# VectorE releases each quad to TensorE, root products move behind quads 24 to 48, and GpSimd waits for its own rows behind every fourth or second quad

## Chip, cores and metric
The kernel runs on one core of a Trainium2 chip. The metric is the device time of one execution in microseconds (us), as the median of several executions. For the kernel before it is 6669.53 us, of 3 executions between 6668.03 and 6680.55 us.

## What is computed
A graph of 3125 nodes with 128 features and 50000 edges (sorted by their target node) goes through four residual blocks; each adds its output to its input and normalises the sum:

```python
x = _layernorm(x + L0(x, edge_index, edge_weight, ...))     # 3 layers: weighted mean of neighbours
x = _layernorm(x + L1(x, edge_index, edge_attr_64, ...))    # message network over nodes and edge features
x = _layernorm(x + L2(x, edge_index, edge_type_8, ...))     # 2 relational convolutions
x = _layernorm(x + L3(x, node_type_16, edge_type_32, ...))  # 2 layers of attention
# in each layer of L0
agg = segment_sum(e_w[:, None] * h[src], dst)
out = relu(agg / clip(segment_sum(e_w, dst), 1) @ w_neigh.T + h @ w_root.T + b_root)   # then a layer norm
# in L2
xt = einsum('ni,rio->nro', x, W);  out = segment_sum(xt[src, etypes], dst) + x @ Wl + b
```

Eight times in all (3 + 1 + 2 + 2 layers) the kernel reads, for every edge, a row of a table by the edge's source, and sums over the edges of each target node.

## The kernel before
**Tiles, quads and steps.** The nodes are 25 blocks of 128 (`NB`). The edges are 391 tiles of 128 (`EDGE_TILES`). One step multiplies one tile of gathered rows with a one-hot matrix (edge by target node within a block) on TensorE and adds the product to a block of an accumulator in PSUM (`accf`, all 25 blocks at once); a tile whose edges reach over two blocks takes two steps, so there are 416 steps. Four tiles are a quad of tiles (98 of them, `TILE_QUADS`), four steps a quad of steps (104, `ALL_QUADS`). `trips` loops over 16 steps (4 quads of steps).

**A gather pass.** All eight passes use `gathers` (L438) on GpSimd: 391 indirect DMAs (L449), one per tile, each of 128 rows, into a ring of 60 tiles (`RING`) in `arena`. Ahead of every fourth tile from tile 60 on it calls `freed`, which waits until the tiles that are to be overwritten have been used (in most passes the semaphore `quad_done` of TensorE). The rows of quad k report to a semaphore `gathered[k % 16]`; `hand_over(k)` waits for it and then counts `arrived` up by one, which is what the consumers wait for. The quad handed over after tile t is the one before the quad just issued, so that GpSimd waits for rows whose transfer was started at least four tiles earlier. The last two are handed over after the loop.

**The order of the passes.** Passes 0, 1 and 2 are the three layers of L0, pass 3 is L1, passes 4 and 5 are the two convolutions of L2, passes 6 and 7 the two attention layers of L3 (`score_phase`). Between two passes the accumulator is turned into the next table, which is stored to memory and must be complete before the next pass gathers from it.

**Passes 0, 1, 2, 4 and 5** are `aggregate_phase` (L654). VectorE makes the one-hots (`onehots`, L427 for all four of a quad at once, L431 one by one where the edge weight is multiplied in), up to 12 quads ahead of TensorE (`DEEP`), and counts `onehot_ready`. TensorE, per quad of steps, waits for `onehot_ready`, then reads from a table in SBUF how many quads of tiles must have arrived (`step_need`, L477, a register load with its checks), waits for `arrived` against that register, and issues four products (L717), each a weight load and a matmul. In pass 0 (`sums`) it also adds the edge weights up, one product per quad (L485). In passes 4 and 5 (`root`) 25 root products (L681, x times Wl, one per block) stand ahead of the quad loop, behind the products that fill the accumulator with the bias (L534).

**Passes 1 and 2** (`edges`, class `EdgeShare`) carry besides, quad by quad, a part of the edge network of L1: TensorE (L816, L835, L822), ScalarE (L856, L867, L871) and VectorE (`mix`, L888) hand each other half a bank, and SyncE loads and stores. `join` calls `mix` for quad n-2 behind the one-hots of quad n; TensorE's products for quad n-2 (`output`, L822) stand in its quad n and wait until quad n-1 is mixed.

**Pass 3** adds the rows on VectorE (L1176) and multiplies on TensorE (L1213). **Passes 6 and 7** gather two rows' width, make scores on VectorE (L1857), and SyncE stores the values (L1840) from the ring, eight transfers per quad; `freed` there waits for these stores too.

## Time and profile before
| | us |
|---|---|
| median of 3 executions | 6669.53 |
| the profiled execution | 6655.79 |
| its span (first to last instruction) | 6654.1 |
| PE busy in it | 3255.9 (49%) |
| DVE busy in it | 2193.3 (33%) |
| ACT busy in it | 1125.8 (17%) |
| POOL busy in it | 3207.3 (48%) |
| DMA packets' mean | 116 GB/s |

PE is TensorE, DVE VectorE, ACT ScalarE, POOL GpSimd, SP SyncE. Register, branch, semaphore and DMA-issuing instructions are not counted as busy, except that POOL's indirect DMAs are (the time in which it makes their descriptors). All of these are means over the whole program, in which the eight gather passes and the stages between them differ; the stretches have to be read one by one.

### The profile page before, as it was taken

The numbers are of one execution on the slowest core, as the hardware profiler recorded it, in microseconds if no ns is written. First come the engines' busy times: TensorE is split into PE (matmuls) and PEld (weight loads), VectorE is DVE, ScalarE is ACT, GpSimd is POOL, SyncE is SP. The second block draws the span as 40 slices with busy tenths as digits, with TensorE's granted clock in tenths as the row PEclk, the third lists the DMA queues.
The fourth block names the chain that finished last, engine by engine and source line by source line (L and its number), as shares of the span: only waits on it lengthen the run. The fifth ranks groups of instructions, "written<-read, shape, count | busy, mean of one in ns | idle before, by whom it ended". The sixth has DMA issues, their size and how long they took to land. (4 is left out here: it accounts for less than half of the span.)

```text
span 6654.1 us, 60476 instructions
## 1 busy us (share of the span) xinstructions
PE 3255.9 (49%) x14685; PEld 2293.0 (34%) x14685; DVE 2193.3 (33%) x5075; ACT 1125.8 (17%) x2416; POOL 3207.3 (48%) x3406
## 2 busy tenths in 40 slices
PE   5444477747773445543353335633334256234353
PEld 3333355534452233332332322223334222233343
DVE  3112222322223223411121114423348544233485
ACT  0000122222222111100010002300114323001053
POOL 4664566446643665366546652066630420666302
PEclk7666676767776667665575557766667677666676
DMA  2111333323332332211131127944434489444343
GB/s 60 47 46 34 79 101 100 93 66 100 102 99 73 94 93 69 106 45 46 42 126 47 46 60 308 408 118 126 128 103 117 137 322 394 117 127 129 99 130 104
DMA packets 600928, 772.14 MB, mean 116 GB/s; under 512 B 89734, under 2 KB 507000, under 8 KB 588064
## 3 DMA queue, kind: packets, MB, share of 16 engines
q1 hardware_dynamic: 480000, 492.16, 22.0%
q0 software_dynamic: 120608, 276.12, 15.6%
q8 instruction: 152, 2.49, 0.2%
q14 instruction: 168, 1.38, 0.1%
HBM read 416.10 MB, written 351.82 MB: 115 GB/s over the span
## 5 line engine op out<-in xcount | busy, mean ns | idle before, releaser
L449 POOL DMA_INDIRECT arena<-table,idx_s x3128 | 2986.5, 955 | 2487.2 <-issue 887.8
L717 PE MATMUL ps<-arena,work 128*128 x4160 | 940.1, 363 | 906.9 <-issue 853.4
L717 PEld LDWEIGHTS ps<-arena,work 128*128 128x128 f32 x4160 | 786.5, 261 | 1163.7 <-issue 1162.0
L431 DVE TENSOR_SCALAR work<-iota_row,dl_s,w_s 128x128 f32<-128x128 f32 x1248 | 347.3, 356 | 446.5 <-remote 330.9
L1897 PE MATMUL ps<-ident,onehot 128*128 128x128 f32 x832 | 193.6, 377 | 614.1 <-DVE onehot L427 385.6
L1857 DVE TENSOR_TENSOR arena<-arena,ps 128x128 f32<-128x128 f32 x832 | 183.8, 282 | 822.1 <-remote 623.2
L427 DVE TENSOR_TENSOR work<-ps,dl_s 128x512 f32<-128x512 f32 x208 | 137.4, 688 | 948.2 <-remote 652.7
L888 DVE SCALAR_TENSOR_TENSOR arena<-ps,vecs,arena 128x256 f32<-128x256 f32 x208 | 100.6, 484 | 965.3 <-ACT arena L867 497.1
L1908 PE MATMUL ps<-arena 128*128 x1664 | 331.4, 363 | 168.3 <-issue 108.7
L1908 PEld LDWEIGHTS ps<-arena 128*128 128x128 f32 x1664 | 298.2, 269 | 201.4 <-issue 198.9
L1897 PEld LDWEIGHTS ps<-ident,onehot 128*128 128x128 f32 x832 | 135.2, 194 | 645.8 <-DVE onehot L427 402.3
L1777 PE MATMUL ps<-arena,work 32*128 32x512 f32 x1600 | 303.5, 887 | 98.3 <-DVE work L1801 45.2
L1805 DVE COPY arena<-ps 128x1024 f32<-128x1024 f32 x200 | 238.8, 1221 | 271.2 <-DMA table<-arena 184.8
L485 PE MATMUL ps<-work,picks 128*104 128x512 f32 x416 | 276.1, 737 | 97.1 <-issue 93.8
L1886 ACT ACTIVATE arena<-ps 128x512 f32<-128x512 f32 x208 | 122.9, 597 | 1140.9 <-remote 658.7
L1612 POOL DMA_INDIRECT sorted_x<-work,pos_i x50 | 48.7, 973 | 548.7 <-DVE work L1704 534.1
L816 PE MATMUL ps<-arena 128*128 128x256 f32 x416 | 190.1, 550 | 219.4 <-issue 112.2
L822 PE MATMUL ps<-arena 128*128 128x128 f32 x832 | 199.4, 378 | 188.1 <-issue 127.3
L1213 PE MATMUL ps<-work,arena 128*128 128x128 f32 x832 | 160.9, 317 | 266.7 <-issue 263.6
L1213 PEld LDWEIGHTS ps<-work,arena 128*128 128x128 f32 x832 | 144.4, 229 | 347.5 <-issue 347.5
L1792 ACT ACTIVATE arena<-ps 128x1024 f32<-128x1024 f32 x200 | 197.9, 1022 | 310.5 <-DMA table<-arena 210.2
L1176 DVE TENSOR_TENSOR arena<-arena 128x128 f32 x416 | 103.8, 289 | 389.2 <-issue 370.2
(329 smaller groups left out, 4077.5 us busy)
## 6 DMA issues: line engine op xcount, KB each, us to landing
table<-arena SPq DMA_DIRECT2D x96, 2048.0 KB
values<-arena SPq DMA_DIRECT2D x832, 64.0 KB
arena<-values SPq DMA_DIRECT2D x208, 256.0 KB
arena<-table,idx_s POOLq DMA_INDIRECT x3128
arena<-edge_times SPq DMA_DIRECT2D x208, 128.0 KB
edge_part<-arena SPq DMA_DIRECT2D x208, 128.0 KB
table<-arena SPq DMA_DIRECT2D x50, 512.0 KB
arena<-edge_part SPq DMA_DIRECT2D x98, 256.0 KB
```

The source lines that it names most:

```text
L431: is_dst = dve.tensor_scalar(home[:, at + c, :], iota, dl_s[:, ds(j + c, 1)], weight[:, ds(j + c, 1)], ALU.is_equal, ALU.mult)
L449: pool.indirect_dma_start(ring[:, ds(t % RING * 2 * H, width)], None, tab, bass.IndirectOffsetOnAxis(ap=idx_s[:, t:t + 1], axis=0)).then_i ...
L485: mm = pe.matmul(quad_sums, picks[:, ALL_QUADS - n:2 * ALL_QUADS - n], deep[:, 4 * (n % DEEP):4 * (n % DEEP) + 4, :].rearrange("p c e -> p ...
L717: mm = pe.matmul(accf[:, ds(b, P)], o, ring[:, ds(slot, H)], start=False, stop=False, skip_group_check=True)
L816: pe.matmul(self.half_b, self.We2, self.hid[:, r, :], start=True, stop=True, skip_group_check=True).then_inc(turned.sem, 1)
L822: mm = pe.matmul(self.half_a[:, c * P:(c + 1) * P], self.ef[:, r, c * P:(c + 1) * P], self.Wn1b, start=True, stop=True, skip_group_check=True)
L1213: mm = pe.matmul(accf[:, ds(b, P)], relu_h[:, (i * U + u) % (4 * RELUS), :], o, start=False, stop=False, skip_group_check=True)
L1777: mm = pe.matmul(ps[:, 4 * kv + g, :], (value_ring if kv else key_ring)[rows, b % 2, :], (pair_v if kv else pair_k)[rows, half * 16:(half ...
L1792: act.activation(rows32[:, m % 3, :, kv * H:kv * H + 64].rearrange("p t (g c) -> p g t c", g=2), ps[:, 4 * kv:4 * kv + 2, :].rearrange("p ...
L1805: dve.tensor_copy(rows32[:, m % 3, :, kv * H + 64:(kv + 1) * H].rearrange("p t (g c) -> p g t c", g=2), ps[:, 4 * kv + 2:4 * kv + 4, :].re ...
L1897: mm = pe.transpose(ps[:, q % 2, c * P:(c + 1) * P], onehot[:, 4 * q + c, :], ident[:, :])
L1908: mm = pe.matmul(ps[:, 4 + q, c * P:(c + 1) * P], onehotT[:, q % 2, c * P:(c + 1) * P], Qn_flat[:, ds(b, P)], start=True, stop=True)
```

## The change
It has five parts. (1) `gathers` gets a number `rest`: behind every `rest`-th quad of tiles it hands over the quad just issued as well, and so waits for its rows before it issues the next DMA. `rest` is 4 in passes 0, 3, 4 and 5 and 2 in passes 1, 2, 6 and 7. (2) In `aggregate_phase` VectorE, behind the one-hots of quad n, reads the need, waits for `onehot_ready` and `arrived` and counts a new semaphore `step_ready` (`release_steps`); TensorE waits for `step_ready` alone, against a constant (in pass 0 for `onehot_ready` too, ahead of the sum). (3) `join` calls `mix` for quad n-1 instead of n-2, behind the release of quad n. (4) The 25 root products stand one by one behind the quads 24 to 48. (5) The base of `step_ready` is moved on after each such pass.

```diff
@@ gathers
-        def gathers(pool, tab, width, freed, joins=None):
+        def gathers(pool, tab, width, freed, joins=None, rest=4):
+            handed = [0]
...
-                if t % 4 == 3 and t >= 7:
-                    hand_over(t // 4 - 1)
-            for k in range((EDGE_TILES - 4) // 4, TILE_QUADS):
+                if t % 4 == 3:
+                    done = t // 4 + 1
+                    for k in range(handed[0], done if done % rest == 0 else done - 1):
+                        hand_over(k)
+                        handed[0] = k + 1
+            for k in range(handed[0], TILE_QUADS):
                 hand_over(k)
...
+        def release_steps(dve, n):
+
+            need = step_need(dve, n)
+            dve.wait_ge(onehot_ready.sem, onehot_ready.at(n + 1))
+            dve.wait_ge(arrived.sem, need + arrived.base)
+            dve.sem_inc(step_ready.sem, 1)
@@ aggregate_phase
-                    gathers(pool, tab, H, freed)
+                    gathers(pool, tab, H, freed, rest=2 if edges else 4)
...
-                    onehots(dve, weight, edges.join if edges else None, iota=None if edges or sums else iota_ps, home=deep)
+                    def then(i, q, first):
+                        release_steps(dve, i * QUADS + q)
+                        if edges:
+                            edges.join(i, q, first)
+                    onehots(dve, weight, then, iota=None if edges or sums else iota_ps, home=deep)
...
-                    if root is not None:
-                        for b in range(NB):
-                            pe.matmul(accf[:, b * P:(b + 1) * P], XT[:, b * P:(b + 1) * P], root, start=False, stop=False,
-                                      skip_group_check=True)
+
+                    def root_product(b):
+
+                        pe.matmul(accf[:, b * P:(b + 1) * P], XT[:, b * P:(b + 1) * P], root, start=False, stop=False, skip_group_check=True)
...
-                                pe.wait_ge(onehot_ready.sem, onehot_ready.at(i * QUADS + u // 4 + 1))
                                 if sums:
+                                    pe.wait_ge(onehot_ready.sem, onehot_ready.at(i * QUADS + u // 4 + 1))
                                     quad_total(pe, i * QUADS + u // 4)
-                                pe.wait_ge(arrived.sem, step_need(pe, i * QUADS + u // 4) + arrived.base)
+                                pe.wait_ge(step_ready.sem, step_ready.at(i * QUADS + u // 4 + 1))
...
                                 mm.then_inc(quad_done.sem, 1)
+                                if root is not None and ROOT_FROM <= i * QUADS + u // 4 < ROOT_FROM + NB:
+                                    root_product(i * QUADS + u // 4 - ROOT_FROM)
@@ EdgeShare
-                if not (first and q < 2):
-                    self.mix(nc.vector, i * QUADS + q - 2, q % 2, not first)
+                if not (first and q < 1):
+                    self.mix(nc.vector, i * QUADS + q - 1, (q - 1) % 2, not (first and q < 3))
...
-                for m in range(ALL_QUADS - 2, ALL_QUADS):
-                    self.mix(dve, m, m % 2, True, m == ALL_QUADS - 1)
+                self.mix(dve, ALL_QUADS - 1, (ALL_QUADS - 1) % 2, True, True)
@@ L1 (pass 3)
-                    gathers(pool, table, H, freed, joins)
+                    gathers(pool, table, H, freed, joins, rest=4)
@@ score_phase (passes 6 and 7)
-                        gathers(pool, table32, 2 * H, freed)
+                        gathers(pool, table32, 2 * H, freed, rest=2)
```

How the instructions stand, in three places. `ISA` are register and semaphore instructions without a name of their own, `xN` is N in a row, and a wait stands on the instruction that follows it.

GpSimd at the start of pass 0 (`rest` 4), before:

```order
L449 DMA arena<-table,idx_s 128x128 x8
L449 DMA arena<-table,idx_s 128x128 [waits gathered0]
L449 DMA arena<-table,idx_s 128x128 x3
L449 DMA arena<-table,idx_s 128x128 [waits gathered1]
L449 DMA arena<-table,idx_s 128x128 x3
L449 DMA arena<-table,idx_s 128x128 [waits gathered2]
```

and now:

```order
L453 DMA arena<-table,idx_s 128x128 x8
L453 DMA arena<-table,idx_s 128x128 [waits gathered0]
L453 DMA arena<-table,idx_s 128x128 x3
L453 DMA arena<-table,idx_s 128x128 [waits gathered1]
L453 DMA arena<-table,idx_s 128x128 x3
L453 DMA arena<-table,idx_s 128x128 [waits gathered2,gathered3]
L453 DMA arena<-table,idx_s 128x128 x7
```

Behind the sixteenth tile the wait is for quads 2 and 3, and quad 3 is the one just issued; then seven DMAs follow before the next wait.

TensorE at the start of pass 4's quad loop, before:

```order
L534 MATMUL ps<-brow,ones 128x128
L681 MATMUL ps<-wts,work 128x128 x25
L465 TENSOR_LOAD blk_i
L466 ISA x2
L472 TENSOR_LOAD slot_i
L473 ISA x2
L477 TENSOR_LOAD need_i [waits onehot_ready]
L477 ISA x2
L711 REGISTER_ALU
L717 ISA [waits arrived]
L717 MATMUL ps<-arena,work 128x128
```

and now at one of the quads 24 to 48:

```order
L735 ISA [waits step_ready]
L735 MATMUL ps<-arena,work 128x128
L735 ISA
L735 MATMUL ps<-arena,work 128x128
L735 ISA
L735 MATMUL ps<-arena,work 128x128
L735 ISA
L735 MATMUL ps<-arena,work 128x128
L700 MATMUL ps<-wts,work 128x128
```

The load of the need, its two checks and the addition are gone from each quad of TensorE, and one root product stands behind each of these 25 quads.

VectorE at the start of pass 0, before (the first twelve quads of one-hots, then one quad at a time):

```order
L431 TENSOR_SCALAR work<-iota_row,dl_s,w_s 128x128 x48
L431 TENSOR_SCALAR work<-iota_row,dl_s,w_s 128x128 [waits quad_done]
L431 TENSOR_SCALAR work<-iota_row,dl_s,w_s 128x128 x3
L431 TENSOR_SCALAR work<-iota_row,dl_s,w_s 128x128 [waits quad_done]
L431 TENSOR_SCALAR work<-iota_row,dl_s,w_s 128x128 x3
```

and now:

```order
L433 TENSOR_SCALAR work<-iota_row,dl_s,w_s 128x128 x4
L484 TENSOR_LOAD need_i
L484 ISA x2
L433 TENSOR_SCALAR work<-iota_row,dl_s,w_s 128x128 [waits onehot_ready,arrived]
L433 TENSOR_SCALAR work<-iota_row,dl_s,w_s 128x128 x3
```

Each quad of one-hots now stands behind the wait for the rows of the quad before it.

## Rows read from the trace of the kernel before

**Rows 1.** The page, busy time by engine and the costliest group.

```profile
PE 3255.9 (49%) x14685; PEld 2293.0 (34%) x14685; DVE 2193.3 (33%) x5075; ACT 1125.8 (17%) x2416; POOL 3207.3 (48%) x3406
...
L449 POOL DMA_INDIRECT arena<-table,idx_s x3128 | 2986.5, 955 | 2487.2 <-issue 887.8
```

**Rows 2.** L449 by pass (0, 1, 3, 4, 6): min/median/max ns, first/last start.

```profile
L449 POOL DMA_INDIRECT arena<-table,idx_s x391: 942/947/1096, 64.4 to 615.2; - x196
...
L449 POOL DMA_INDIRECT arena<-table,idx_s x391: 942/947/1070, 682.2 to 1267.4; - x196
...
L449 POOL DMA_INDIRECT arena<-table,idx_s x391: 943/947/1393, 2066.6 to 2626.1; - x196
...
L449 POOL DMA_INDIRECT arena<-table,idx_s x391: 942/947/3378, 2734.3 to 3300.7; - x196
...
L449 POOL DMA_INDIRECT arena<-table,idx_s x391: 943/949/975, 4325.4 to 4925.6; - x196
```

**Rows 3.** Who POOL waited for in pass 4: us in total, times, longest.

```profile
POOL arena L449 <- issue: 107.9, 354, 0.3
...
POOL arena L449 <- remote: 52.5, 13, 5.5
POOL arena L449 <- PE ps L717: 24.2, 5, 19.5
```

**Rows 4.** Timeline of pass 4 (start us, us, engine, line), around a stall.

```profile
2935.13 0.37 PE L717 MATMUL ps<-arena,work 128*128 x1 [1.74 <-issue]
...
2937.89 0.95 POOL L449 DMA_INDIRECT arena<-table,idx_s  x1 [0.31 <-issue]
2938.62 0.37 PE L717 MATMUL ps<-arena,work 128*128 x1 [3.12 <-issue]
2939.32 0.29 PEld L717 LDWEIGHTS ps<-arena,work 128*128 128x128 f32 x1 [2.51 <-issue]
...
2942.13 0.37 PE L717 MATMUL ps<-arena,work 128*128 x1 [1.04 <-issue]
2942.82 0.29 PEld L717 LDWEIGHTS ps<-arena,work 128*128 128x128 f32 x1 [1.11 <-issue]
2943.52 4.72 PE L717 MATMUL ps<-arena,work 128*128 x19 [1.02 <-issue]
...
2943.79 0.94 POOL L449 DMA_INDIRECT arena<-table,idx_s  x1 [4.96 <-remote]
```

**Rows 5.** L717 in passes 0, 1, 4: busy us, mean ns, idle before.

```profile
L717 PE MATMUL ps<-arena,work 128*128 x832 | 168.4, 319 | 244.0 <-issue 242.5 <-POOLq L445 0.9
...
L717 PE MATMUL ps<-arena,work 128*128 x832 | 184.0, 359 | 3.4 <-issue 3.4
...
L717 PE MATMUL ps<-arena,work 128*128 x832 | 201.2, 392 | 321.0 <-issue 288.6 <-DVE work L427 25.5 <-POOLq L445 6.0
```

**Rows 6.** Timeline of pass 0, a short pause of POOL.

```profile
204.05 0.95 POOL L449 DMA_INDIRECT arena<-table,idx_s  x1 [1.63 <-issue]
...
208.71 0.37 PE L717 MATMUL ps<-arena,work 128*128 x1 [1.73 <-issue]
...
211.51 1.23 PE L717 MATMUL ps<-arena,work 128*128 x5 [1.02 <-issue]
```

**Rows 7.** Timeline of pass 1, a short pause of POOL.

```profile
916.47 0.95 POOL L449 DMA_INDIRECT arena<-table,idx_s  x1 [1.38 <-remote]
...
918.36 0.47 ACT L867 ACTIVATE arena<-ps,vecs 128x256 f32<-128x256 f32 x1 [6.24 <-remote]
```

**Rows 8.** DMA, 40 slices of 3301.5 to 3304, behind pass 4's last gather.

```profile
DMA  0000000000000969040201000000000000000000
```

**Rows 9.** Who POOL waited for, pass 6.

```profile
POOL arena L449 <- DMA values<-arena: 91.6, 21, 16.7
```

**Rows 10.** Lines of pass 4 and of pass 1: busy us, mean ns, idle.

```profile
L427 DVE TENSOR_TENSOR work<-ps,dl_s 128x512 f32<-128x512 f32 x104 | 68.8, 688 | 472.2 <-remote 338.6 <-PE ps L717 114.6 <-issue 18.8
...
L681 PE MATMUL ps<-wts,work 128*128 128x128 f32 x50 | 10.5, 368 | 16.8 <-issue 16.6
...
L431 DVE TENSOR_SCALAR work<-iota_row,dl_s,w_s 128x128 f32<-128x128 f32 x414 | 116.4, 353 | 0.0
```

More of the change, by code:

```diff
@@ L54 @@
 RELUS = 10
+ROOT_FROM = 24
 class Signal:
@@ L176, in build @@
         onehot_ready = signal("onehot_ready")
+        step_ready = signal("step_ready")
         quad_done = signal("quad_done")
@@ L746, in aggregate_phase @@
             gather_pass_over()
+            step_ready.base += ALL_QUADS
             if sums:
```

## Prediction

> **What bounds the kernel now.** I first read the page. No engine is half busy [rows 1], but line L449, the indirect DMAs of GpSimd (POOL), has 3128 pieces of 955 ns, 2986 us of a span of 6654. So I went through the program by gather pass. One gather costs 947 ns, and where POOL waits for nothing there are 107.9 / 354 = 0.305 us between two [rows 2, 3]. A pass of 391 gathers issued back to back would last 390 x 1.252 = 488.3 us from the first start to the last. The passes take 550.8 (0), 585.2 (1), 559.5 (3), 566.4 (4) and 600.2 us (6) [rows 2]; pass 2 is built as 1, pass 5 as 4, pass 7 as 6, and I count them the same. Over the floor they are 62, 97, 71, 78 and 112 us. This excess, some 695 us over all eight, is what the change can win or enlarge; the stages between the passes it leaves alone.
>
> What is the excess? In pass 4 it is 52.5 us of waits ended by a remote event and 24.2 us for TensorE's products [rows 3]: both are `freed`, which waits for tiles of the ring to be used up. So TensorE, whose work is small, is late. The timeline shows how [rows 4]: while POOL issues, TensorE does one load or matmul and then idles 1 to 3 us, put down to "issue", that is to nothing that the trace sees. Its steps are multiples of 0.70 us (2938.62 to 2939.32, 2942.13 to 2942.82 to 2943.52). POOL has been quiet from 2938.84, and at 2943.52, 4.7 us later, TensorE suddenly does 19 matmuls in 4.7 us. Over pass 4 this is 288.6 us of idle time ended by "issue" ahead of 832 matmuls, in pass 0 242.5 us [rows 5]. I call it the slow mode: with POOL issuing without a break, another engine's sequencer goes down to one instruction per 0.7 us. In pass 1, where TensorE does more, the same line idles 3.4 us in all [rows 5]. What differs is that POOL there stops every four to eight tiles, for 1.2 to 2.5 us. One such case: POOL stands still from 915.1 to 916.5, and ScalarE, held for 6.24 us by an event that came late, goes on at 918.36 although POOL is issuing again [rows 7]. So a short stop seems to release what was held. Against it stands pass 0: a stop of 1.63 us before 204.05 did not end a slow stretch that lasted until 211.51 [rows 6]; but that stretch had been let grow first.
>
> **Part 1, the waits for own rows.** Behind pass 4's last gather (start 3300.7, end 3301.6) packets move until slice 22 of 40, 3302.9 us [rows 8], 1.2 to 1.3 us. A wait for the rows just issued takes that plus the way back to POOL, in place of the usual 0.305 us: at least 0.9 us more, at most about 1.5; I take 1.2. In passes 0, 3, 4 and 5 there are 24 such waits: 29 us each, floor 488.3 + 29 = 517. In passes 1, 2, 6 and 7 there are 48: 57.6 us, floor 546. SP's and the other queues carry nothing behind POOL, but every consumer waits for `arrived`, which POOL counts; the quad just issued is now handed over earlier than before (before its four successors), the others as before.
>
> What they may win: with a stop each 16 tiles (20 us) or each 8 (11 us), TensorE has few instructions between two stops, and the slow mode, which ends at each long stop and comes again while POOL issues, should not set in. Then the stalls of `freed` go, as TensorE is short of nothing else. I leave 4 us per pass for what remains. Pass 0: 551 - 521 = **30**. Pass 3: 559.5 - 521 = **38**. Passes 1 and 2: 585 - 550 = 35 each, **70**. Passes 4 and 5: 566.4 - 521 = 45 each, **90** (with parts 2 and 4). Passes 6 and 7 wait for SyncE's stores, 91.6 us [rows 9]. SyncE is held in the same way but within a few tiles, so stops every eight tiles end it and do not prevent it; between nothing (600) and all (550) I take 585, nearer the row of before: 15 each, **30**.
>
> **Part 2, VectorE releases.** TensorE loses four register instructions of some 25 records per quad. In the slow mode that is 2.8 us of a quad, outside it nothing, since POOL's 5.0 us per quad (4 x 1.252) covers it. VectorE gains about seven. Its one-hots are 0.69 us per quad (pass 4) or 4 x 0.353 = 1.4 us (pass 1) [rows 10], `mix` under 0.5. The register load has no row on VectorE: between 0 and, at 0.7 us for each of seven, 4.9 us. I take 1 us, as an engine that isn't slow spends well under 0.2 us on such an instruction between TensorE's matmuls of rows 4's fast stretch. Sum 1.4 + 1.0 + 0.5 = 2.9 of 5.0 us: covered. If the cover goes (the 4.9), 1.4 + 4.9 + 0.5 = 6.8 us per quad, and VectorE is the bound. The one-hots ahead of time are lost: what waits behind VectorE's wait is the next quad's one-hots and `mix`, at most 1.9 us behind the rows, inside the 5 us until the next rows. 0.
>
> **Part 3, mix one quad earlier.** It stays opposite TensorE's products of the same quad, without which VectorE, no longer ahead, would hold TensorE. 0.
>
> **Part 4, root products.** Line L681's 50 records (25 products, some in two passes of the array) cost 10.5 us and 16.8 us of idle ahead of pass 4's first quad [rows 10]; POOL pays for it with the 19.5 us at tile 60 [rows 3]. That stall is part of the 45 above. Placed behind quads 24 to 48 they add about 0.4 us to quads that have 5 us. 0 more.
>
> **Sum.** 30 + 38 + 70 + 90 + 30 = 258 us. Against the profiled execution: 6655.8 - 258 = 6398. The median of the runs shown is 13.7 us above that execution; with it, **6410 us**.
>
> **Rivals.**
> (a) *The stops take the place of stalls, but the slow mode stays.* For it: rows 6, and 4.7 us from POOL's stop to TensorE's recovery in rows 4, where a stop of 1.5 us is three times shorter. Then the 29 us of stops are absorbed in the 62 to 78 us of waits, TensorE is quicker only by its missing instructions, and passes 4 and 5 save most of the 19.5 us: some 2 x 25 + 2 x 15 = 80 us, 6590.
> (b) *Nothing much*: absorbed, and the late root products and VectorE's releases eat the rest: within 13 us of 6669.5 (62 us of excess in pass 0 less 29 of stops is a bound on what may be left over there, and in pass 1 97 less 57.6, so that little is left once VectorE's part costs a third of it).
> (c) *The stops come on top: slower.* The place is the loop of POOL and ring in the four passes with `rest=2` above all. If late events still come, and each stop is added in full, that is 4 x 57.6 + 4 x 28.8 = 346 us; the half of it, with the gain of 80 from (a) kept, gives 6670 + 173 - 80 = 6763. It decides when a stop removes less than it costs: 1.2 us per 8 tiles is 57.6 of the 97 us of excess in pass 1, so over 40% of the excess must stay; in pass 0, 29 of 62. For it: pass 1 shows no slow mode on line L717 now, so its stops have less to cure. Against: pass 1's existing waits are of the stop's own length and can merge with it. The Trainium skill speaks for this rival: "DMA: Bandwidth & Descriptors", § Rules for kernel authors, has a DMA issued early and its semaphore waited for late, so that the fixed cost overlaps. The change does the opposite at every drain; by that rule alone the whole 346 would be lost. Rows 4 show why I give it little: POOL idles 4.96 us in one go there already, four times what a stop adds.
> (d) *VectorE becomes the bound: slower.* If its register instructions fall into the slow mode, 104 quads of steps at 6.8 us are 707 us in passes 1 and 2 instead of 550, and at 1.4 + 4.9 us 655 us in pass 0 instead of 521: 6410 + 2 x 157 + 134 = 6858. Against: with stops, nobody should be slow.
>
> **Numbers.** Forecast 0.66 (own range 6330 to 6520), (a) 0.12, (b) 0.07, (c) 0.10, (d) 0.05. A measurement of this kernel can tell about 0.2% (13 us) from no change. Faster: 0.66 + 0.12 = 0.78; same 0.07; slower 0.15. The forecast's low end: all 288 stops at 0.9 instead of 1.2 us give 86 us more, 6324, and passes 6 and 7 may win more than 15 each; the range runs from 6300 to 6680, over (a) and (b), and leaves out (c), (d) and little else.
>
> **What would show it.** Right: line L449's passes at about 521 (0, 3, 4, 5), 550 (1, 2) and 585 us (6, 7); TensorE's idle ended by "issue" ahead of line L735 down from 243 and 289 us to under 60, most of its idle being for VectorE's release; no wait of POOL for TensorE at tile 60 over 5 us; stops of 1.5 us. Wrong: pauses of 4 to 5 us still there between the stops (a, c), VectorE's one-hots 0.7 us apart or later than the rows (d).

## The result: 6504.27 us, 0.975 of before

The changed kernel takes 6504.27 us (median of 4 executions, 6496.06 to 6516.86), the kernel before 6668.78 us beside it (4 executions, 6666.06 to 6680.55). The ratio is 0.9751, 95% interval 0.9734 to 0.9769: 164.5 us faster. 260 had been forecast, and 6410 us. The profiled execution of the change takes 6516.86 us, its span is 6515.1 us, 139.0 less than that of the profiled execution before. What is read from the traces below therefore adds up to 139 us, not to 164.5.

From here on "slow mode" is what the prediction calls so: one instruction per 0.7 us on TensorE, VectorE or SyncE while POOL issues. One thing has to be known to read all that follows. The kernel before took about 6669, 6722 and 6666 us on three of the occasions on which kernels were run for this document, and 5758, 5758 and 5760 us on three others. The traces on the first three show the slow mode, those on the others do not. The result above belongs to the first kind. On record are chips 8 and 4 for the other two occasions with the slow mode, chip 7 once and chip 11 twice for those without it, and none for the result above. The kernel before was traced with the slow mode only; without it, its time and the traces of its variants are known.

### The profile after

The page's busy lines of the change, in answer to [rows 1]:

```profile
PE 3454.9 (53%) x14685; PEld 2426.0 (37%) x14685; DVE 2199.7 (34%) x5075; ACT 1126.3 (17%) x2416; POOL 3210.2 (49%) x3406
...
L453 POOL DMA_INDIRECT arena<-table,idx_s x3128 | 2989.8, 956 | 2458.4 <-issue 995.9
```

TensorE is busy 199 us longer for the same 14685 matmuls; POOL's gathers cost the same. "Issue" ahead of them has grown from 888 to 996 us, which holds a part of the stops; most are put down to line L453's own DMAs, 477 us in 218 waits. Line L453 (the old L449) by pass, 0, 1, 3, 4 and 6, as in [rows 2] (min/median/max ns, first and last start):

```profile
L453 POOL DMA_INDIRECT arena<-table,idx_s x391: 938/944/1094, 64.3 to 618.2; - x196
...
L453 POOL DMA_INDIRECT arena<-table,idx_s x391: 938/944/1052, 678.2 to 1274.1; - x196
...
L453 POOL DMA_INDIRECT arena<-table,idx_s x391: 938/944/1489, 2010.0 to 2575.1; - x196
...
L453 POOL DMA_INDIRECT arena<-table,idx_s x391: 938/944/3577, 2661.9 to 3222.0; - x196
...
L453 POOL DMA_INDIRECT arena<-table,idx_s x391: 940/946/972, 4229.8 to 4837.9; - x196
```

First start to last start is 553.9, 595.9, 565.1, 560.1 and 608.1 us, where it was 550.8, 585.2, 559.5, 566.4 and 600.2. The forecast had 521, 550, 521, 521 and 585. So the passes have hardly moved, most of them the wrong way. The whole program by pass, worked out from the starts and ends of that line (pass: first start to last end; rest: from there to the next pass's first gather, or the end):

| pass | before: pass + rest | after: pass + rest | difference |
|---|---|---|---|
| 0 | 551.8 + 66.0 | 554.9 + 59.0 | -3.9 |
| 1 | 586.1 + 97.1 | 596.9 + 54.7 | -31.6 |
| 2 | 589.1 + 112.1 | 603.5 + 76.7 | -21.0 |
| 3 | 560.4 + 107.3 | 566.1 + 85.8 | -15.8 |
| 4 | 567.3 + 77.7 | 561.1 + 70.8 | -13.1 |
| 5 | 562.6 + 383.5 | 552.4 + 383.6 | -10.1 |
| 6 | 601.2 + 723.5 | 609.1 + 688.2 | -27.4 |
| 7 | 603.6 + 400.4 | 615.2 + 372.8 | -16.0 |

The eight passes together are 37 us **longer**, and the rests between them 176 us **shorter**. The time was won where the prediction said that the change leaves everything alone. Of the 139 us, passes 1, 2, 3, 6 and 7 with their rests have 112, and 0, 4 and 5 have 27.

Why, is seen behind the last gather of a pass. Before, what TensorE still has to do then, in pass 1 (L717) and pass 3 (L1213), and what SyncE still has to store in pass 6 (L1840): count, min/median/max ns, first and last start. Each product is two of these matmuls, so 116 are 58 steps, about a full ring.

```profile
L717 PE MATMUL ps<-arena,work x116: 275/275/581, 1268.8 to 1321.7; 128*128 x116
...
L1213 PE MATMUL ps<-work,arena x140: 269/275/417, 2626.9 to 2658.7; 128*128 128x128 f32 x140
...
L1840 SPq DMA_DIRECT2D values<-arena x59: 4/331/2065, 4928.0 to 4973.3; - x59
```

And after, the same lines under their new numbers:

```profile
L735 PE MATMUL ps<-arena,work x20: 275/421/581, 1275.2 to 1285.1; 128*128 x20
...
L1233 PE MATMUL ps<-work,arena x24: 275/275/422, 2575.8 to 2582.9; 128*128 128x128 f32 x24
...
L1860 SPq DMA_DIRECT2D values<-arena x11: 4/329/341, 4838.9 to 4846.1; - x11
```

116 matmuls that end 53 us behind the last gather have become 20 that end 10 us behind it; 140 (32 us) have become 24 (7 us); 59 stores (47 us) have become 11 (7 us). Before, GpSimd ended a pass with a ring full of rows that nobody had used. Now the consumers have kept up, and since the next pass's table needs the last product, this is worth its full length. They have not only ended closer to GpSimd but earlier: from a pass's first gather to the end of its last product, pass 1 takes 640 us before and 607 now.

The slow mode itself, by line of TensorE (busy, mean ns, idle before): first the kernel before, in pass 1 ahead of the edge network's products and in pass 3:

```profile
L822 PE MATMUL ps<-arena 128*128 128x128 f32 x408 | 98.5, 381 | 84.9 <-issue 60.0 <-DVE arena L888 24.9
...
L816 PE MATMUL ps<-arena 128*128 128x256 f32 x206 | 95.2, 555 | 116.2 <-issue 63.4 <-ACT arena L856 52.0
...
L1213 PE MATMUL ps<-work,arena 128*128 128x128 f32 x832 | 160.9, 317 | 266.7 <-issue 263.6 <-ACT arena L1191 3.1
```

Then the change, for L735 in passes 0, 1 and 4 as in [rows 5], and for L1233 in pass 3:

```profile
L735 PE MATMUL ps<-arena,work 128*128 x832 | 172.4, 332 | 204.2 <-issue 203.3
...
L735 PE MATMUL ps<-arena,work 128*128 x832 | 196.4, 378 | 73.7 <-issue 47.4 <-DVEq L529 26.3
...
L735 PE MATMUL ps<-arena,work 128*128 x832 | 193.4, 373 | 321.6 <-issue 310.1 <-DVEq L529 10.5
...
L1233 PE MATMUL ps<-work,arena 128*128 128x128 f32 x832 | 174.2, 374 | 229.4 <-ACT arena L1211 144.3 <-issue 85.1
```

In passes 0 and 4 it is still there, with the stops: 203 and 310 us of "issue" idle (243 and 289 before). In pass 3, "issue" is down from 264 to 85 us, and TensorE waits most for ScalarE. In pass 1 the slow mode was there before as well, though not ahead of L717, the line that the prediction looked at (3.4 us): it stood ahead of L816 and L822. All of TensorE's idle time ended by "issue", from a pass's first gather to its last, for passes 0 to 7: 288, 127, 121, 307, 296, 326, 164 and 168 us before; 269, 80, 47, 93, 318, 316, 69 and 62 in the change. It has gone down by 37 to 70% in passes 1, 2, 3, 6 and 7, and by 7% at most, if at all, in 0, 4 and 5. (Without the slow mode, the change has 49 us in pass 0 and 1 to 7 in the others.) What POOL waited for in pass 4, in answer to [rows 3]:

```profile
POOL arena L453 <- issue: 138.5, 366, 2.5
...
POOL arena L453 <- PE ps L735: 12.7, 5, 4.0
POOL arena L453 <- remote: 8.1, 4, 4.1
```

The remote waits went from 52.5 to 8.1 us and the products' from 24.2 to 12.7 with 4.0 us as the longest instead of 19.5, but "issue" rose by 31 and the waits for line L453's own rows from 5.5 to 25.2: the stops stand where the stalls stood. One stop in pass 3's timeline:

```profile
2146.48 0.94 POOL L453 DMA_INDIRECT arena<-table,idx_s  x1 [0.30 <-issue]
2149.76 0.94 POOL L453 DMA_INDIRECT arena<-table,idx_s  x1 [2.34 <-DMA arena<-table,idx_s]
2151.01 0.94 POOL L453 DMA_INDIRECT arena<-table,idx_s  x1 [0.30 <-issue]
```

The gap is 2.34 us instead of 0.30: a stop costs **2.04 us** more, not 1.2. Over all stops of the change the median gap is 2.37 to 2.44 us in passes 0 to 5 and 2.73 in passes 6 and 7, whose rows are twice as wide. The transfer took 1.2 to 1.3 us behind pass 4's last gather [rows 8]; if it takes as long here, some 1.1 us pass between its last packet and the next gather's start.

### The profile page after: what moved, and what is told of

Same layout as the page of the kernel before. It is cut to its first block and busy times, and to the rows that moved or that the text cites. A ratio compares the mean times of both kernels' runs of the same rounds, so it can differ in the third digit from the quotient of the medians.

```text
span 6515.1 us, 60996 instructions
## 1 busy us (share of the span) xinstructions
PE 3454.9 (53%) x14685; PEld 2426.0 (37%) x14685; DVE 2199.7 (34%) x5075; ACT 1126.3 (17%) x2416; POOL 3210.2 (49%) x3406
## 5 line engine op out<-in xcount | busy, mean ns | idle before, releaser
L453 POOL DMA_INDIRECT arena<-table,idx_s x3128 | 2989.8, 956 | 2458.4 <-issue 995.9
L735 PE MATMUL ps<-arena,work 128*128 x4160 | 968.1, 370 | 953.0 <-issue 884.8
L735 PEld LDWEIGHTS ps<-arena,work 128*128 128x128 f32 x4160 | 815.3, 269 | 1207.8 <-issue 1207.4
L1917 PE MATMUL ps<-ident,onehot 128*128 128x128 f32 x832 | 217.7, 413 | 671.5 <-DVE onehot L429 543.5
L1928 PE MATMUL ps<-arena 128*128 x1664 | 391.4, 413 | 5.1 <-issue 3.6
L1928 PEld LDWEIGHTS ps<-arena 128*128 128x128 f32 x1664 | 352.7, 313 | 26.5 <-issue 17.1
L492 PE MATMUL ps<-work,picks 128*104 128x512 f32 x416 | 320.8, 857 | 77.8 <-issue 76.8
L1233 PE MATMUL ps<-work,arena 128*128 128x128 f32 x832 | 174.2, 374 | 229.4 <-ACT arena L1211 144.3
L843 PE MATMUL ps<-arena 128*128 128x128 f32 x832 | 218.1, 407 | 135.5 <-DVE arena L909 95.4
L1233 PEld LDWEIGHTS ps<-work,arena 128*128 128x128 f32 x832 | 149.6, 269 | 368.1 <-issue 368.1
```

The source lines that it names most:

```text
L453: pool.indirect_dma_start(ring[:, ds(t % RING * 2 * H, width)], None, tab, bass.IndirectOffsetOnAxis(ap=idx_s[:, t:t + 1], axis=0)).then_i ...
L492: mm = pe.matmul(quad_sums, picks[:, ALL_QUADS - n:2 * ALL_QUADS - n], deep[:, 4 * (n % DEEP):4 * (n % DEEP) + 4, :].rearrange("p c e -> p ...
L735: mm = pe.matmul(accf[:, ds(b, P)], o, ring[:, ds(slot, H)], start=False, stop=False, skip_group_check=True)
L843: mm = pe.matmul(self.half_a[:, c * P:(c + 1) * P], self.ef[:, r, c * P:(c + 1) * P], self.Wn1b, start=True, stop=True, skip_group_check=True)
L1233: mm = pe.matmul(accf[:, ds(b, P)], relu_h[:, (i * U + u) % (4 * RELUS), :], o, start=False, stop=False, skip_group_check=True)
L1917: mm = pe.transpose(ps[:, q % 2, c * P:(c + 1) * P], onehot[:, 4 * q + c, :], ident[:, :])
```

## The experiments

Each takes the changed kernel as its base, unless it says otherwise. `RESTS` gives `rest` by pass, and 1000 means no stop; every other part of the change is kept. The runs stand in order; kernels of one occasion share the executions of the kernel before.

### No stops; stops alone; root products ahead; other stops by pass

```diff
+RESTS = [1000, 1000, 1000, 1000, 1000, 1000, 1000, 1000]
@@ gathers
+        passes = [0]
...
+            rest = RESTS[passes[0]]
+            passes[0] += 1
             handed = [0]
```

> The changed kernel without any wait for own rows (the rest is kept: VectorE's releases, mix a quad earlier, late root products). Theory S (the stops keep the other engines quick, so that nobody is behind when GpSimd has done its last gather): most of the 164 us are lost, 6600 to 6680 us; TensorE ends over 25 us behind the last gather again in passes 1, 2 and 3, and SyncE over 35 us behind in passes 6 and 7. Rival R (TensorE's fewer instructions bring the gain, and the stops only cost): about as fast as the change or faster, 6300 to 6520 us.

The second has the kernel before as its base, with the new loop of `gathers` and `RESTS = [4, 2, 2, 4, 4, 4, 2, 2]`, and nothing else of the change.

> The kernel before with the stops alone (4 quads in passes 0, 3, 4, 5, 2 in 1, 2, 6, 7). Theory S: passes 3, 6 and 7 as in the changed kernel, since the change does nothing else there; passes 1 and 2 close to it; in all 6500 to 6600 us. Rival R: slower than before, 6680 to 6800 us.

```diff
@@ aggregate_phase (third kernel)
                     fill_rows(pe, row)
+                    if root is not None:
+                        for b in range(NB):
+                            root_product(b)
...
-                                if root is not None and ROOT_FROM <= i * QUADS + u // 4 < ROOT_FROM + NB:
-                                    root_product(i * QUADS + u // 4 - ROOT_FROM)
```

> The changed kernel with the 25 root products ahead of the quad loop again, as before. Both theories: only passes 4 and 5 move, by 5 to 20 us each; the stall of GpSimd at tile 60 grows from 3.4 us in pass 4 to over 8 us. In all 6510 to 6540 us.

```diff
+RESTS = [1000, 1000, 4, 2, 1000, 2, 4, 3]
```

> The changed kernel with other stops by pass: none in passes 0, 1 and 4, behind every fourth quad in 2 and 6, every third in 7, every second in 3 and 5. A look at each pass from its first gather to the next pass's. Theory S: pass 1 without stops 20 to 35 us longer than the 651.6 us of the change; pass 2 about the same or 10 us shorter than 680.2; pass 6 between 1297 (change) and 1325 (before); pass 0 and 4 without stops within 10 us of the change's 613.9 and 631.9, as TensorE's steps of 0.7 us are still there with stops; pass 5 with twice as many stops either loses TensorE's 0.7 us steps and is 5 to 25 us shorter, or is up to 40 us longer. Rival R: passes 0, 1 and 4 without stops 20 to 60 us shorter.

Measured: the kernel before 5758.40 us (13 executions, 5755.47 to 5764.98). Without stops 5759.53 us, ratio 1.0001 (0.9991 to 1.001). The stops alone on the kernel before 6426.48 us, 1.1157 (1.1139 to 1.1176). Root products ahead 6425.73 us, 1.1152 (1.1133 to 1.1171). Other stops by pass, one execution, 6147.74 us.

All four expectations missed, since all had 6669 us in mind. Line L458 of the kernel without stops, in passes 1 and 6:

```profile
L458 POOL DMA_INDIRECT arena<-table,idx_s x391: 940/944/1057, 600.6 to 1089.3; - x196
...
L458 POOL DMA_INDIRECT arena<-table,idx_s x391: 942/946/972, 3727.8 to 4215.3; - x196
```

488.7 and 487.5 us from first to last start: the floor of 390 x 1.252 = 488.3 that the prediction worked out, without one stall. Passes 3 (517.0) and 4 (494.5) have no stall either; some of their gathers are longer. Its TensorE in passes 0 and 4:

```profile
L740 PE MATMUL ps<-arena,work 128*128 x832 | 163.2, 359 | 138.2 <-DVEq L534 138.2
...
L740 PE MATMUL ps<-arena,work 128*128 x832 | 203.1, 425 | 246.6 <-DVEq L534 241.9 <-issue 4.7
```

4.7 us of "issue" in pass 4 instead of 289 [rows 5]; TensorE waits for VectorE's release. In the timeline of pass 4 the release comes from VectorE right behind the rows, and all of a quad's eight matmuls follow within 2.07 us while POOL issues:

```profile
2506.06 0.69 DVE L430 TENSOR_TENSOR work<-ps,dl_s 128x512 f32<-128x512 f32 x1 [4.26 <-POOLq L454]
...
2506.13 2.07 PE L740 MATMUL ps<-arena,work 128*128 x8 [3.43 <-DVEq L534]
...
2507.19 0.95 POOL L458 DMA_INDIRECT arena<-table,idx_s  x1 [0.30 <-issue]
```

So on this chip there was nothing for a stop to mend. TensorE's granted clock is not what tells the two kinds apart: in pass 4 its mean was 0.58 of full speed in the trace of before, with the slow mode, and 0.52 here. The kernels then differ by their stops alone: 668.1 us for the 288 stops on the kernel before, 2.32 us each; (6147.74 - 5759.53) / 176 = 2.21 us each for those of the fourth kernel. The other parts (VectorE's releases, `mix`, the late root products) are worth nothing here, 5759.5 against 5758.4, and whether the root products stand ahead or behind makes no difference (6425.7 against 6424.1 and 6415.7 for the change, below): POOL never gets to wait for the ring.

### The change and no stops, once more

> The changed kernel itself, since in the first four runs the kernel before took 5758 us where it had taken 6669, and showed no slow mode. If that belongs to the chip (or to its condition at the time) and not to the kernels, there are two cases. Without the slow mode: before about 5758 us, the change about 6420 us, 288 stops at 2.1 to 2.4 us more each. With it: before about 6669 us, the change about 6500 us.

> The changed kernel without stops, beside the change itself. Without the slow mode: equal to before, about 5758 us. With it: theory S says 6600 to 6680 us, with TensorE over 25 us and SyncE over 35 us behind the last gather; rival R, by which TensorE's fewer instructions brought the gain, says 6300 to 6520 us.

Another chip, and again no slow mode. The change 6415.71 us, ratio 1.1143 (1.1125 to 1.1162) to a before of 5758.34; without stops 5756.86 us, 0.9998 (0.9988 to 1.0007). The difference of the two is 658.9 us, 2.29 us a stop. Who POOL waited for in pass 0 of the change there:

```profile
POOL arena L453 <- issue: 106.7, 344, 0.9
POOL arena L453 <- DMA arena<-table,idx_s: 63.5, 46, 2.5
```

The own rows' waits are put down to line L453's DMAs, 63.5 us with 2.5 as the longest, and beside "issue" and the wait ahead of the pass's first gather there is no other entry. So the change that made this kernel 2.5% faster on one occasion makes it 11.4% slower on another, and its stops are all of the loss. What they cost by pass can be read here without a disturbance: against the kernel without stops, 2.1 us a stop in passes 0, 4 and 5, 2.2 in 1 and 2, 1.9 in 3, and 2.6 in 6 and 7.

### Stops in some passes only, and a later wait in two

```diff
+RESTS = [1000, 1000, -2, 1000, 1000, -4, 1000, 2]
...
-                if t % 4 == 3:
-                    done = t // 4 + 1
-                    for k in range(handed[0], done if done % rest == 0 else done - 1):
+                if t % 4 == (0 if rest < 0 else 3):
+                    done = (t + 1) // 4
+                    for k in range(handed[0], done if done % abs(rest) == 0 else done - 1):
```

> The changed kernel without stops in passes 0, 1, 3, 4 and 6, with them behind every second quad in 7, and in 2 and 5 with a wait for own rows that stands one gather later (behind the first gather of the next quad; every second quad in 2, every fourth in 5). First to last gather start of each pass, and the way to the next pass's first. If the chip shows no slow mode: 488 us in passes 0, 1, 4 and 6, about 518 in pass 3; 613 in pass 7; with the later wait a stop costs about 0.9 instead of 2.1 us, as one gather's 1.25 us lie in it: some 532 us in pass 2, 510 in pass 5. If it does: theory S says pass 3, without stops, has its 0.7 us steps on TensorE and VectorE again and ends 25 us behind the last gather, pass 6 has SyncE over 35 us behind and pass 7 under 10; rival R says passes 1, 4 and 6 are quicker than in the change.

This chip showed the slow mode: before 6721.74 us (3 executions), this 6657.23 us (2), ratio 0.9903 (0.9869 to 0.9936). Passes 1, 3, 4 and 6, all without stops:

```profile
L458 POOL DMA_INDIRECT arena<-table,idx_s x391: 938/944/1053, 679.8 to 1270.3; - x196
...
L458 POOL DMA_INDIRECT arena<-table,idx_s x391: 938/944/1441, 2071.2 to 2638.5; - x196
...
L458 POOL DMA_INDIRECT arena<-table,idx_s x391: 938/944/3808, 2751.2 to 3310.5; - x196
...
L458 POOL DMA_INDIRECT arena<-table,idx_s x391: 940/946/972, 4319.8 to 4944.8; - x196
```

What TensorE still had to do behind the last gather in pass 1 (no stops) and pass 2 (the later wait), and, in a fence of its own, what SyncE had in pass 7 (stops as in the change):

```profile
L740 PE MATMUL ps<-arena,work x112: 275/275/582, 1275.5 to 1325.7; 128*128 x112
...
L740 PE MATMUL ps<-arena,work x112: 275/275/377, 1960.6 to 2009.4; 128*128 x112
```

```profile
L1865 SPq DMA_DIRECT2D values<-arena x9: 14/331/341, 6279.3 to 6286.5; - x9
```

The way from first gather to next pass's first gather, against the change:

| pass | this kernel | stops here | change | before |
|---|---|---|---|---|
| 0 | 614.8 | none | 613.9 | 617.8 |
| 1 | 689.6 | none | 651.6 | 683.2 |
| 2 | 701.8 | later wait | 680.2 | 701.2 |
| 3 | 680.0 | none | 651.9 | 667.7 |
| 4 | 631.9 | none | 631.9 | 645.0 |
| 5 | 936.7 | later wait | 936.0 | 946.1 |
| 6 | 1346.3 | none | 1297.3 | 1324.7 |
| 7 | 984.7 | as the change | 988.0 | 1004.0 |

The last two columns are from another occasion, on which the kernel before is 53 us quicker, so differences of a few microseconds mean nothing. Those of passes 1, 3 and 6 do: without stops they take 38, 28 and 49 us longer, with TensorE 55 us (pass 1) and SyncE 46 us (pass 6) behind the last gather, as before the change. TensorE's idle time ended by "issue" is back as well: 314 us in pass 3 and 151 in pass 6, while pass 7, which kept its stops, has 70. (Pass 1, at 97 us, lies between the change's 80 and the 127 of before.) Theory S holds there, and rival R falls: with all of TensorE's instructions saved, pass 1 is no quicker than before. In passes 0, 4 and 5 the stops do nothing. Line L740 in pass 4 without stops:

```profile
L740 PE MATMUL ps<-arena,work 128*128 x761 | 171.0, 358 | 320.9 <-issue 319.0 <-DVEq L534 1.7
```

319 us of "issue" without stops and 310 with them. The 13 and 10 us that passes 4 and 5 have won come without stops in pass 4 and with the later wait in pass 5 too, hence from the releases and the late root products together; the two were not separated with the slow mode present.

The later wait costs less. In pass 5 the gap behind it is 1.03 to 1.19 us in 18 of 24 cases, some 0.8 more than the usual 0.30 and less than half of a full stop's price, since a gather's issue lies in it. In pass 2 it is worth nothing: 112 matmuls are left behind the last gather, as without stops. Why the later wait does not help and the full stop does, this run can't tell. It may be the length, or that no transfer is under way at the end of a full stop; and quads between two such waits are handed over one gather later than before as well.

### A shorter lead, and late stops

If the gain lies behind the last gather, it can be had without a stop, by not letting GpSimd run so far ahead.

```diff
+LEAD = 36
+RESTS = [1000, 1000, 1000, 1000, 1000, 1000, 1000, 1000]
...
-                if t % 4 == 0 and t >= RING:
-                    freed(pool, (t - RING + 3 + NB - 1) // 4)
+                if t % 4 == 0 and t >= LEAD:
+                    freed(pool, (t - LEAD + 3 + NB - 1) // 4)
```

> The changed kernel without stops, and GpSimd at most 36 tiles (less the blocks' 27) ahead of the products instead of 60. What stops win with the slow mode is won behind the last gather; a shorter lead should win the same without stops: the end of a pass leaves at most 9 quads of steps to do instead of 15, some 20 us less behind each of passes 1, 2, 3, 6 and 7. With the slow mode: 80 to 130 us faster than before, with the passes themselves within 10 us of e7's without stops. Rival: with less lead the slow stretches of TensorE stop GpSimd sooner, the passes get 10 to 30 us longer, and nothing is won. Without the slow mode: equal to before, 5758 us, since consumers are only a quad or two behind.

The second keeps the ring's lead of 60 and the change's numbers, with `if done % rest == 0 and t >= 288` in place of `if done % rest == 0`.

> The changed kernel with its stops only from tile 288 on, the last quarter of each pass. If the gain is that the engines have caught up when GpSimd ends, a quarter of the stops is enough for it. With the slow mode: as fast as the change or up to 40 us faster (6460 to 6520 where before is 6669), TensorE and SyncE under 25 us behind the last gather in passes 1, 2, 3, 6 and 7. Rival: a stop only keeps an engine quick and does not let it catch up: tails over 35 us, 6600 us. Without the slow mode: a quarter of the change's loss, some 5925 us.

The slow mode was there; before 6665.77 us (7 executions). Short lead 6560.69 us, 0.9837 (0.9821 to 0.9854). Late stops 6585.85 us, 0.9883 (0.9867 to 0.99). TensorE behind pass 1's last gather, first with the short lead, then with the late stops:

```profile
L741 PE MATMUL ps<-arena,work x68: 275/275/581, 1261.6 to 1293.3; 128*128 x68
```

```profile
L740 PE MATMUL ps<-arena,work x92: 275/275/421, 1271.0 to 1313.3; 128*128 x92
```

With the short lead 68 matmuls are left instead of 116, and TensorE ends 34 us behind instead of 54; in pass 6 SyncE ends 27 us behind instead of 47, in pass 7 28 instead of 43. The passes hold their length where it was in question (589.8 us in pass 1, 586.1 before), though passes 6 and 7 and 3 are 10 us longer: a gain of 105 us (under 2%, but with an interval clear of none), within the 80 to 130 that were expected. It did not come as expected, though: that was 20 us in each of passes 1, 2, 3, 6 and 7. The late stops missed their number: 6460 to 6520 was expected. 92 matmuls are left in pass 1 (43 us); of those five passes only pass 3 has its tail down to 9 us, after six stops. In passes 1 and 2 twelve late stops did not make up for a full ring. Where the time went, as differences from the kernel before in the way from first gather to next pass's first gather, worked out from the traces:

| pass | 0 | 1 | 2 | 3 | 4 | 5 | 6 | 7 | sum |
|---|---|---|---|---|---|---|---|---|---|
| short lead | -13.0 | -15.1 | -17.4 | +4.6 | -17.4 | -17.0 | -6.0 | -2.8 | -84 |
| late stops | -3.6 | -3.9 | +3.0 | -13.2 | -17.8 | -18.1 | -13.7 | -8.1 | -75 |
| the change | -3.9 | -31.6 | -21.0 | -15.7 | -13.2 | -10.1 | -27.4 | -15.9 | -139 |

Both kernels keep VectorE's releases and the late root products, and passes 4 and 5, which win 35 us in either, win most of that without any stop or short lead (13 and 10 in the run above). In passes 1, 2, 3, 6 and 7 the short lead wins 37 us, the late stops 36 and the change 112. So between a half and two thirds of the short lead's gain is the lead's own (46 to 58 of the 84 us in the traces), and that the number fell into its range is in part luck. The full stops, from the start of a pass, do more than shorten the tail: they also make the consumers quicker, as the "issue" idle times of the change show.

### Both together, on a chip without the slow mode

`LEAD = 36` with `RESTS = [1000, 2, 2, 4, 1000, 1000, 2, 2]`; the short lead alone; and the change.

> The short lead of 36 tiles in all passes and the change's stops in passes 1, 2, 3, 6 and 7 alone, where they were worth something with the slow mode. With it: passes 0, 4 and 5 as with the short lead alone (604.9, 627.6 and 929.1 us to the next pass, 4 to 9 us under the change each), the others as in the change: 10 to 30 us faster than the change, 6475 to 6495 where before is 6669. Rival: the two don't add, since a pass with stops has no stall of the ring left and passes 0, 4 and 5 vary by as much: within 5 us of the change. Without the slow mode: 216 stops at 2.1 to 2.4 us, about 6240 us.

> The short lead without stops once more (every other part of the change kept). Without the slow mode: equal to before, 5758 us. With it: 0.984 of before again.

> The change itself beside the two. With the slow mode 0.975 of before again, without it 1.114.

No slow mode: before 5760.12 us (13 executions). Both together 6273.72 us, 1.0891 (1.0872 to 1.0909); the 216 stops cost 516.0 us more than the short lead alone, 2.39 each (about 6240 us was expected, at 2.1 to 2.4 a stop; 192 of them stand in passes with `rest` 2, half of these in passes 6 and 7, where a stop costs most). The short lead alone 5757.68 us, 0.9998 (0.9988 to 1.0007). The change 6424.06 us, 1.1147 (1.1128 to 1.1165). Whether both together beat the change with the slow mode was not seen.

This ran on the same chip as the second group of runs, and both times the slow mode was absent.

## Why the prediction was right, and where not

**The number came out for a reason other than the one given, and that is luck.** 6504 us lies in the forecast's own range of 6330 to 6520, at its upper end. Forecast: 260 us from shorter passes. Measured: passes 37 us longer, the rests between them 176 us shorter. The sentence that failed is "the stages between the passes it leaves alone". The stages are the same, but their start is the consumers' last product, and how far that lies behind the last gather was a number in the trace (116 matmuls left in pass 1) that the prediction didn't look at. Two errors met: stops at nearly twice their price took away what the passes should have won, and the tails, put at nothing, gave 176 us back. Luck was also that the slow mode was there at all: on the three occasions without it the change would have been, or was, 11% slower.

**Part 1, price of a stop.** Taken at 1.2 us between 0.9 and 1.5; it is 2.04 us in pass 3 and 2.2 to 2.4 us on average over whole kernels. The mis-sized term is "the way back to POOL": 1.1 us where a few tenths were thought. What a pass with its stops takes when nothing disturbs it is measured in the change without the slow mode, from first to last start: 538.6, 595.0, 594.6, 563.0, 545.5, 538.8, 612.5 and 612.7 us for passes 0 to 7, where 517 and 546 were thought. With the slow mode passes 1, 3, 6 and 7 (595.9, 565.1, 608.2, 614.3) take that within 5 us, pass 2 (602.7) 8 more, and 0, 4 and 5 (554.0, 560.2, 551.5) 13 to 15 more. So even where the slow mode was gone nothing could be won within a pass: pass 1's 97 us over its floor became 108, nearly all stops.

The excess that this was to win was 707 us over all eight passes by the prediction's own figures (62, twice 97, 71, twice 78, twice 112), not the 695 that it gives; the forecast doesn't use that sum.

**Part 1, the effect.** "The slow mode should not set in": it became rarer in passes 1, 2, 3, 6 and 7 (TensorE's "issue" idle down by 37 to 70%), enough to shorten their tails; it stayed in 0, 4 and 5, where "issue" ahead of L735 was still 203 us (0) and 310 (4; under 60 was forecast) and stops are worth nothing. The argument leant on a misreading: pass 1 was taken to be nearly free of the slow mode because of its short pauses, while it had 123 us of it ahead of lines L816 and L822. By pass (forecast, measured with the rests): 0: 30, 4; 3: 38, 16; 1 and 2: 70, 53; 4 and 5: 90, 23; 6 and 7: 30, 43.

**Part 2** cost nothing, as forecast: with VectorE releasing, no stops and no slow mode, six of the eight passes sit on the floor of 488 us, and the whole kernel takes as long as before. What TensorE's fewer instructions brought with the slow mode is small where it can be seen alone: 3 to 4 us in pass 0. **Part 3**: 0, in agreement with the kernel without stops, though it wasn't tried alone. **Part 4**: the stall at tile 60 of pass 4 went from 19.5 to 3.4 us as said (to 9.4 in the kernel without stops there), but only 13 us of pass 4 went with it; the rest was taken by later waits and the stops.

**The rivals.** (a) describes passes 0, 4 and 5. (c) describes the chips without the slow mode: its upper end, all stops in full, was put at 346 us and is 659 there. The rule of the Trainium skill ("DMA: Bandwidth & Descriptors", § Rules for kernel authors: issue early, wait late) holds in full there. With the slow mode it is outweighed. The kernel with the short lead wins two thirds of the gain without breaking it, a good part of that through the releases and late root products. (d) fell: no pass of any run shows VectorE as the bound. That one and the same kernel could have two lengths 14% apart was no rival at all, and it turns the verdict round.

**What stays open.** What makes a chip show the slow mode. Nothing in the kernels or in the counts of the page does it: the change was traced with and without, with 187 and 144 packets on the two instruction queues both times. Whether it is the chip or its condition at the time is not settled either; the one chip that came twice was without it both times. The stops alone and the root products ahead ran only without the slow mode, so what each part is worth with it is known for the stops by pass and for the rest only together.

## What to carry to other kernels

Where a producer runs ahead through a ring, look at what is left to do behind its last piece: slow consumers are paid for there, in full, and stalls within the loop may be no more than the producer waiting for its own surplus. Try a bound on how far ahead it may run before making it wait for itself: here the shorter lead cost nothing where the consumers kept up (5757.7 against 5760.1 us), though it won less than its total suggests where they didn't. And before a cost is paid against a disturbance (a stop, a wait, a drain), find out whether the disturbance is there on every chip that the kernel will run on; here the remedy was worth 2.5% with it and cost 11% without it.

## What the runs showed of the hardware

- One instruction per 0.7 us on TensorE, VectorE and SyncE while GpSimd issues indirect DMAs without a pause. In the trace of before, TensorE's steps in pass 4 are in [rows 4]; VectorE's register loads and their checks in pass 3 start at 2198.61, 2199.31 and 2200.71 us, and SyncE's instructions in pass 6 at 4430.51, 4431.21, 4431.91, 4432.61 and 4433.30. Seen on three occasions, absent on three others, with the change on both kinds. The kernel before takes 911 us more on the first (6669 against 5758).
- Waiting for the rows of the DMA just issued costs GpSimd 2.1 us more than going on where a row has 128 numbers, and 2.4 where it has 256 (medians of the change), 2.2 to 2.4 as an average over whole kernels; the packets of pass 4's last gather had landed 1.2 to 1.3 us after its issue ended.
- A wait one gather later costs some 0.8 us more than none (gaps of 1.03 to 1.19 us), and in pass 2 did not help against the slow mode, where the full stop did.
